# Cross attention's P and V as half-precision pairs, with the products of two heads on the two column halves of the array

## The reference

```python
q = (xn @ w_q).reshape(B, SQ, NUM_HEADS, DIM_HEAD)
kv = context @ w_kv
k, v = jnp.split(kv, 2, axis=-1)
scores = jnp.einsum('bqhd,bkhd->bhqk', q * SCALE, k)
attn = jax.nn.softmax(scores, axis=-1)
out = jnp.einsum('bhqk,bkhd->bqhd', attn, v).reshape(B, SQ, INNER)
out = out @ w_out + b_out
return out * jnp.tanh(gate[0])
```

## Time and profile before

| | |
|---|---|
| median of 3 runs | 815.51 us (809.0 to 815.84) |
| the profiled execution | 821.01 us, its span 819.2 us |
| entries 0 to 7, first score product of each at | 105.4, 165.0, 229.8, 294.6, 359.5, 424.3, 489.2, 554.0 us |
| last product of the attention block, about | 618 us |
| PE, DVE, ACT, POOL busy | 80%, 66%, 50%, 27% of the span |
| granted TensorE clock, mean of the span | 0.895 of 2.4 GHz |

### The profile page before, as it was taken

How to read it: one execution, slowest core, us unless ns; L and a number is a source line. 1 busy time by engine, 2 the same in 40 slices (tenths; PEclk the granted TensorE clock), 3 DMA queues, 4 the chain that set the end, 5 groups by cost and what they waited for, 6 DMA issues and landing times. The chain is left out here.

```text
span 819.2 us, 13429 instructions
## 1 busy us (share of the span) xinstructions
PE 653.4 (80%) x4168; PEld 524.3 (64%) x4168; DVE 540.7 (66%) x1124; ACT 412.3 (50%) x1021; POOL 218.1 (27%) x223
## 2 busy tenths in 40 slices
PE   5717679889889898899889888988767864789980
PEld 4516468678678687777777777867665452456650
DVE  3974367886886787787786787786756851963332
ACT  2414175584585566476466456555533621853431
POOL 3540031231231232132232133122212530133331
PEclk9955689999999999999999999999956986999995
DMA  9113200200110210210210110040216444533324
GB/s 285 46 38 123 62 1 12 77 26 8 56 51 0 61 51 0 61 51 0 51 61 0 37 50 26 11 128 28 78 52 209 144 147 138 174 60 58 53 33 102
DMA packets 55634, 54.24 MB, mean 66 GB/s; under 512 B 17256, under 2 KB 44976, under 8 KB 55600
## 3 DMA queue, kind: packets, MB, share of 16 engines
q1 hardware_dynamic: 51504, 48.61, 19.5%
q0 software_dynamic: 4096, 5.19, 4.0%
HBM read 43.67 MB, written 10.13 MB: 66 GB/s over the span
## 5 line engine op out<-in xcount | busy, mean ns | idle before, releaser
L582 POOL TENSOR_TENSOR probs<-probs,c_rcp 112x750 f32<-112x750 f32 x64 | 92.0, 1437 | 321.3 <-DVE c_rcp L942 321.3
L705 ACT ACTIVATE probs<-ps_s,c_neg 112x375 f32<-112x375 f32 x128 | 72.5, 578 | 30.4 <-DVE c_neg L934 30.1
L1243 PE MATMUL ps_t<-ident,probs 112*125 112x112 f32 x384 | 55.6, 282 | 22.0 <-DVE cpt_lo L946 22.0
L1243 PEld LDWEIGHTS ps_t<-ident,probs 112*125 112x125 f32 x384 | 50.2, 194 | 29.0 <-issue 25.3
L131 PE MATMUL ps_o<-ctxt_hi,w_k_lo 128*128 128x376 f32 x128 | 49.5, 387 | 19.4 <-DVE oct_lo L821 19.2
L613 ACT ACTIVATE kt_hi<-ps_o 128x376 fp32r<-128x376 f32 x64 | 31.4, 490 | 60.8 <-PE ps_o L133 60.8
L1543 POOL DMA_INDIRECT moe_sum<-gsh_hi,xs_in x21 | 33.3, 1585 | 106.3 <-DMA moe_sum<-gsh_hi,xs_in 64.0
L932 DVE TENSOR_REDUCE c_max<-ps_s 112x2 f32<-112x750 f32 x64 | 59.8, 935 | 2.2 <-PE ps_s L133 1.3
L131 PE MATMUL ps_o<-cpt_hi,v_lo 125*128 125x224 f32 x192 | 58.5, 305 | 2.8 <-DVE kt_lo L821 1.7
L946 DVE TENSOR_TENSOR cpt_lo<-ps_t,cpt_hi 125x672 fp32r<-125x672 f32 x64 | 54.7, 855 | 9.0 <-ACT cpt_hi L613 8.9
L613 ACT ACTIVATE oct_hi<-ps_o 64x112 fp32r<-64x112 f32 x128 | 33.0, 258 | 54.4 <-PE ps_o L133 52.9
(11 more groups left out here) (289 smaller groups left out, 1914.7 us busy)
## 6 DMA issues: line engine op xcount, KB each, us to landing
chunk<-in_L_ffn_ew_dram SPq DMA_DIRECT2D x24, 512.0 KB, 3.6
spare<-in_L_ffn_ew_dram SPq DMA_DIRECT2D x18, 512.0 KB
store<-in_L_ffn_ew_dram SPq DMA_DIRECT2D x6, 512.0 KB, 6.0
ctx_raw<-in_ctx_dram SPq DMA_DIRECT2D x8, 375.0 KB
moe_in<-chunk SPq DMA_DIRECT2D x1, 2709.0 KB, 14.1
xs_in<-moe_in SPq DMA_DIRECT2D x21, 129.0 KB
plain_raw<-in_L_xattn_w_kv_dram SPq DMA_DIRECT2D x2, 1024.0 KB, 14.5
store<-in_L_ffn_sw_dram SPq DMA_DIRECT2D x3, 512.0 KB, 6.6
```

The lines of the kernel that those rows point to most:

```text
L582: pool.tensor_tensor(p, p, r, ALU.mult).then_inc(sg["p_normed"], 1)
L705: act.activation(probs[:, s % 2, h, :], ps_s[0:N, h, 0:SK], ACT.Exp, bias=c_neg[:, s % 2, h:h + 1], scale=CROSS_SCALE, accum_out=c_sum[:, ...
L1243: last = pe.transpose(ps_t[0:SKT, h, t * N:(t + 1) * N], probs[:, s % 2, h, t * SKT:(t + 1) * SKT], ident[0:N, 0:N])
```

## The change

P and V of cross attention become pairs of fp16 parts in place of fp32r parts, with the same three products. fp16 has a small range, so the values are scaled by powers of two first. P is multiplied with 2^14 (an immediate of the instructions that split it). V's scale is computed on the chip from a bound on V: the greatest absolute value of V's weights times the greatest sum of absolute values in a piece of the context. `gate_v` takes both scales back out after `cross_out`.

`pv` issues each product by head: 64 columns of stationary V and 112 moving columns of the head's own P. Head 0's go to partitions 0 to 63 of `ps_o`, head 1's to partitions 64 to 127, on the array's column halves. These are 18 matmuls in place of 9, in the order head 0, head 1 for each product. The result is 128 x 112, and `o_hi` and `o_lo` take it out with one instruction each.

To find the scale there are new steps. In the preparation block these are two DMAs of the whole context (3 MB), eight ACT passes over it with sums (125 x 768 each), a DVE maximum over V's raw weights (128 x 2048) and a small one over the sums. At the start of the attention block these are two small transposes and ten small DVE instructions. The V weights are loaded second instead of fifth, and the first projection no longer waits for the second part of x. The preparation block's semaphores are cleared and reused by the later blocks, behind one more meeting of all engines.

```diff
@@ preparation_block
+            load_x(0, slice(0, 2))
+            load_plain(2)
+            load_x(1, slice(2, B))
+            for i in (0, 1, 3):
+                load_plain(i)
             sp.dma_start(raw[:, 6:8, :], ...)
+            for h in range(2):
+                sp.dma_start(ctx_all[:, 12 * h:12 * h + 12, :],
+                             A["ctx"][4 * h:4 * h + 4].rearrange("b (t p) d -> p (b t) d", p=SKT)).then_inc(sg[f"ctx_all{h}"], 16)
...
+            for b in range(B):
+                act.wait_ge(sg[f"ctx_all{b // 4}"], 16)
+                entry = ctx_all[:, ST * b:ST * b + ST, :].rearrange("p t d -> p (t d)")
+                act.activation(entry, entry, ACT.Abs, accum_out=ctx_sum[:, b:b + 1]).then_inc(sg["ctx_sum"], 1)
...
+            dve.wait_ge(sg["plain2"], 16)
+            dve.tensor_reduce(v_cols[:, 1:2], plain_raw[2][:, :], X, ALU.max, apply_absolute_value=True).then_inc(sg["v_cols"], 1)
@@ attention_block
-        v = pair("v", [SKT, 2, ST, 512])
+        v = half_pair(nc, ctx, "v", [SKT, 2, ST, 512])
-        cpt = pair("cpt", [SKT, 2, ST, N])
+        cpt = half_pair(nc, ctx, "cpt", [SKT, 2, ST, N])
...
-                hi(v[0][:, q, t, :], ps_v[0:SKT, :]).then_inc(sg["v_hi"], 1)
+                act.activation(v[0][:, q, t, :], ps_v[0:SKT, :], ACT.Copy, scale=v_scale[0:SKT, 0:1]).then_inc(sg["v_hi"], 1)
...
-                for h in range(2):
-                    r = slice(64 * h, 64 * h + 64)
-                    hi(oct_[0][r, s, :], ps_o[r, h * N:(h + 1) * N]).then_inc(sg["oct_hi"], 1)
+                hi(oct_[0][:, s, :], ps_pv).then_inc(sg["oct_hi"], 1)
...
                 for t in range(ST):
-                    last = product(pe, ps_o[:, 0:2 * N], tuple(w[:, s // 4, t, c] for w in v),
-                                   tuple(w[:, :, t, :] for w in cpt), start=t == 0, stop=t == ST - 1)
+                    for n, (a, w) in enumerate(((1, 0), (0, 1), (0, 0))):
+                        for h in range(2):
+                            at = (s % 4) * P + h * CHD
+                            last = pe.matmul(ps_pv[h * CHD:(h + 1) * CHD, :], v[a][:, s // 4, t, at:at + CHD], cpt[w][:, h, t, :],
+                                             start=t == 0 and n == 0, stop=t == ST - 1 and n == 2)
                 last.then_inc(sg["pv_full"], 1)
...
             preparation_block(nc, signals[0], A, ident, consts, weights, qk_rot, v_all, v_cols)
+            signals[0].clear()
```

More of the change, by code:

```diff
@@ L117, in __getitem__, with clear, release @@
         if name not in self.sems:
-            self.sems[name] = self.ctx.enter_context(self.nc.semaphore(self.block + "_" + name))
+            self.sems[name] = self.nc.alloc_semaphore(name=self.block + "_" + name)
         return self.sems[name]
+    def clear(self):
+        handles = list(self.sems.values())
+        self.nc.clear_and_free_semaphores(handles)
+        self.held = [self.nc.alloc_semaphore(name=f"{self.block}_held{i}", num=h.num) for i, h in enumerate(handles)]
+    def release(self):
+        for h in self.held:
+            self.nc.release_semaphore(h)
 def later(count):
@@ L138, in split_pair, with half_pair @@
     return tuple(ctx.enter_context(nc.sbuf_tensor(f"{name}_{part}", shape, F32R)) for part in ("hi", "lo"))
+def half_pair(nc, ctx, name, shape):
+    return tuple(ctx.enter_context(nc.sbuf_tensor(f"{name}_{part}", shape, F16)) for part in ("hi", "lo"))
 def product_over_width(pe, out, lhs, w, cols):
@@ L146, in product_over_width, with preparation_block @@
     return last
-def preparation_block(nc, sg, A, ident, consts, weights, qk_rot, v_all):
+def preparation_block(nc, sg, A, ident, consts, weights, qk_rot, v_all, v_cols):
     w_k, w_v, w_q, w_o, w_proj = weights
@@ L364, in _ @@
             pe.wait_ge(sg["wt_lo"], 4)
+            project(0, 0)
             pe.wait_ge(sg["x_loaded1"], 16)
-            for b0 in range(B // 2):
+            x_transpose(2, 0)
+            project(1, 1)
+            x_transpose(3, 1)
+            for b0 in range(1, B // 2):
                 if b0 < B // 2 - 1:
@@ L392, in expert_weights, with attention_block @@
     return tuple(A[n][e] for n in ("ew1", "ew2", "ew3"))
-def attention_block(nc, sg, A, x2_all, ident, consts, weights, qk_rot, v_all, raw, ffn_sg, w_max, gw_raw, xs):
+def attention_block(nc, sg, A, x2_all, ident, consts, weights, qk_rot, v_all, raw, ffn_sg, w_max, gw_raw, xs, v_cols):
     w_k, w_v, w_q, w_o, w_proj = weights
@@ L465, in ctx_bank @@
             return bank(f"C{k}") if later(b) else ps_s[:, k, :]
+        ps_k = ps_o[:, 0:SKP]
+        ps_pv = ps_o[:, 0:N]
         stack = work[:, :].rearrange("p (t b r c w) -> p t b r c w", t=2, b=B, r=2, c=4)
@@ L543, in _ @@
         def _(pool):
+            pool.memset(v_mask[:, :], float("inf")).then_inc(sg["masked"], 1)
             pool.memset(chunk[:, 0:D + 1], 0.0).then_inc(sg["zeroed"], 1)
@@ L688, in k_hi @@
                     act.wait_ge(sg["s_full"], PAIRS * b + p - 1)
-                hi(kt[0][:, p % 2, :], ps_o[:, 0:SKP]).then_inc(sg["kt_hi"], 1)
+                hi(kt[0][:, p % 2, :], ps_k).then_inc(sg["kt_hi"], 1)
             def v_hi_cross(b, f):
@@ L711, in cpt_hi @@
                     act.wait_ge(sg["pv_full"], PAIRS * b + s)
-                hi(cpt[0][:, :, :, :].rearrange("p h t n -> p h (t n)"), ps_t[0:SKT, :, 0:ST * N]).then_inc(sg["cpt_hi"], 1)
+                act.activation(cpt[0][:, :, :, :].rearrange("p h t n -> p h (t n)"), ps_t[0:SKT, :, 0:ST * N], ACT.Copy,
+                               scale=P_SCALE).then_inc(sg["cpt_hi"], 1)
             def o_hi(b, s):
@@ L953, in o_lo @@
             def o_lo(b, s):
-                for h in range(2):
-                    dve.wait_ge(sg["oct_hi"], 2 * (PAIRS * b + s) + h + 1)
-                    r = slice(64 * h, 64 * h + 64)
-                    lo(oct_[1][r, s, :], ps_o[r, h * N:(h + 1) * N], oct_[0][r, s, :]).then_inc(sg["oct_lo"], 1)
+                dve.wait_ge(sg["oct_hi"], PAIRS * b + s + 1)
+                lo(oct_[1][:, s, :], ps_pv, oct_[0][:, s, :]).then_inc(sg["oct_lo"], 1)
             def x2_moments(b):
@@ L1203, in k_project @@
                 if later(PAIRS * b + p - 4):
-                    pe.wait_ge(sg["oct_lo"], 2 * (PAIRS * b + p - 4))
+                    pe.wait_ge(sg["oct_lo"], PAIRS * b + p - 4)
                 m = slice(p * P, (p + 1) * P)
                 for k in range(KD):
-                    last = product(pe, ps_o[:, 0:SKP], tuple(t[:, k, m] for t in w_k), tuple(t[:, k, :] for t in ctxt),
+                    last = product(pe, ps_k, tuple(t[:, k, m] for t in w_k), tuple(t[:, k, :] for t in ctxt),
                                    start=k == 0, stop=k == KD - 1)
@@ L1265, in cross_out @@
                     pe.wait_ge(sg["v_lo"], v_before_output(b))
-                pe.wait_ge(sg["oct_lo"], 2 * (PAIRS * b + pairs[-1] + 1))
+                pe.wait_ge(sg["oct_lo"], PAIRS * b + pairs[-1] + 1)
                 for k in pairs:
@@ L1294, in fill @@
                     q_transpose(b, int(f[1]))
-            for f in FILLS[:FILLS.index("T1") + 1] + ["C0", "C1", "O0", "T2"]:
+            pe.transpose(ps_v[0:2, 0:P], v_cols[:, :], ident[:, :]).then_inc(sg["v_scale_full"], 1)
+            fill(0, "QA")
+            fill(0, "QB")
+            pe.wait_ge(sg["v_scaling"], 3)
+            pe.transpose(ps_v[:, P:P + 2], v_row[:, :].to_broadcast([2, P]), ident[0:2, 0:2]).then_inc(sg["v_scale_full"], 1)
+            for f in FILLS[2:FILLS.index("T1") + 1] + ["C0", "C1", "O0", "T2"]:
                 fill(0, f)
+            pe.wait_ge(sg["v_scaling"], 4)
             k_project(0, 0)
```

61 lines of the change are left out of this document (48 added, 13 removed).

## The result

The changed kernel took 792.62 us (median of 4 runs, 789.59 to 796.29) against 812.25 (4 runs, 808.17 to 815.84) for the kernel before: 0.9738 of its time, 95% interval 0.9687 to 0.9789. In a second set it took 792.33 against 816.29, 0.9756 (0.9669 to 0.9844). So it is 20 to 24 us faster. The forecast was 29.3 us and 786; the range 766 to 813 holds the result. The forecast was made off 815.51, the median of three runs. Every ratio in this document is to the kernel before in the same set of runs and leaves out slow runs, those over 1.5% above the fastest of their kernel.

The account below looks back on a forecast made before the run. It took the loop PE (`pv`), ACT and DVE (`oct`), DVE's other work, PE again as the bound. 25.6 + 11.5 - 2.2 - 3.2 + 1.6 - 4 = 29.3 us off 815.5 gives 786; range 766 to 813.

Parts of the forecast that it names:

- the loop PE, ACT, DVE: A step runs through PE (`pv`), ACT and DVE (`oct`), DVE's other work, PE again; the change shortens `pv` and `oct`.
- Both serial rivals: `pv` halves run one after the other: 816, 12%; the same, with weights not loading beside a running matmul: 845, 8%.
- PE: In `pv`, 9 groups at 0.055 plus 0.19 take 0.69 instead of 1.08: 25.6 us saved over 64 pairs.
- 0.19 for the split: Cost in `pv` of going into a split array and moving on to `scores`, both charged: 0.19 us.
- the terms (25.6 - 3.2 + 1.6 = 24.0 of 25.6): `pv` saves 25.6 us, less 3.2 in steps where PE idles, plus 1.6 at entry 7's low clock.
- The way out: Taking `pv`'s result out loses one instruction of 0.27 from the chain; two thirds on the path, 11.5 us.
- The bound of 17.3: Saving on taking the result out if the lost instruction lay on the path in all 64 pairs: 17.3 us.
- One sign named ahead: In the profile after, PE's wait for `oct_lo` would be well under 19 us.
- What gets dearer: In the loop, `v_hi` reads its scale from a tile, 687 ns against 598: -2.2 us; DVE's `lo` charged nothing.
- The start's share of 4: Before the loop, the scale's new steps and the meeting of engines cost 4 us, bounds 0 and 8.
- the 0.8 for the meeting: Before the loop, the cleared semaphores add a meeting of the engines: 0.8 us, taken unseen.
- The step without a gain: In one step of eight PE idles because DVE does the next self softmax before `oct_lo`: -3.2 us.

Follow-up runs that it names:

- the second profile of before: The kernel before, unchanged, run again for another profile: 812.35 us (10 runs), entries of 61.8 us without a low stretch.

## Why the prediction was right, and where it was off

**The mechanism was right**: both halves run at once, the way out is one instruction shorter, and the loop PE, ACT, DVE passes on all of the second and a part of the first. Both serial rivals fell with the timeline. That the profiled spans differ by 29.7, almost the 29.3 forecast, is luck in part: 2.6 of it lies behind attention, and the terms err both ways. By its terms:

- **PE.** 0.055 a group and 0.19 for the split were 0.05 and about 0.13 (the first distance 0.08, the last 0.15), so the block was 0.57 and not 0.69. But at most 0.7 of the saving arrives, where the terms (25.6 - 3.2 + 1.6 = 24.0 of 25.6) had nearly all. By the product 0.51 x 64 x 0.7 = 23 and the two errors cancel; by the entries less arrives, and the term was too large.
- **The way out** was mis-sized: 17 us and not 11.5. The bound of 17.3 was the right value. I had counted PE's waits for `oct_lo`; where PE doesn't wait there, DVE's `cpt_lo` and what follows come earlier instead, and PE waits for those. One sign named ahead did not come: the wait for `oct_lo` was to be well under 19 us, and it is 17.1 (19.2 before), in 21 waits instead of 32. PE comes to it earlier.
- **What gets dearer.** `v_hi` as priced (689 ns for 687). "DVE's `lo` becomes a two-operation form ... I charge nothing" was right of the form and wrong of the scale from a tile, 60 ns. Together with the start it is 8 us by the product, charged were 6.2. The start's share of 4 was right (3.9) as a whole; its parts, the 0.8 for the meeting among them, no run shows.
- **The step without a gain** was there, 12.85 and 12.84. Its reason, DVE's order, was only half of it: ACT's exponentials are late next.
- **Not foreseen:** step 7 gives 0.5 back. The chain `xn`, `xnt_hi`, `xnt_lo` on DVE and ACT didn't get shorter, so PE comes earlier and waits: 1.71 for `xnt_lo`, where the second profile of before has 1.08 (before, then after):

```profile
284.18 0.49 PE L131 MATMUL ps_a<-w_q_hi,xnt_lo 128*112 128x512 f32 x1 [1.08 <-DVE xnt_lo L821]
```

```profile
341.77 0.49 PE L143 MATMUL ps_a<-w_q_hi,xnt_lo 128*112 128x512 f32 x1 [1.71 <-DVE xnt_lo L873]
```

- **The clock is the step that failed.** The prediction priced a low stretch well (1.6, measured 1.5), but took the profiled execution's two an entry for the kernel's own, and then "the steps get shorter as well, so PE's share stays about the same". Before's other profile has fewer, about one an entry, and the mean clock of its runs fits that (0.903, against 0.895 in the first profile); the changed kernel has two. The one in step 4 went, another came in step 7, behind exactly the wait that had grown. That is some 10 us, a good third of what the clock's rival named (26). Without it the change brings 30 to 32 us, against the 29.3 of the sum; with it 20 to 24.

Open is what decides where the stretches fall. The experiments show that filling PE's idle time removes them or moves them, not more. Open too is 2.6 us of the profiled difference after attention (201.6 to 199.0), where the changed code does nothing. Over all profiles, of either kernel and its variants, this stretch varies from 197 to 202 us, so it may be chance.

## What to carry to other kernels

Two independent products with 64 stationary columns each, on the column halves, cost what one does, and the result then lies in one block that one instruction takes out; count in full the instruction that this saves, where it stands in the loop. Compare kernels by span times granted clock beside the time, from several runs, before saying what an edit of 1 or 2% does: here the clock hid a loss of 5 to 8 us once and made another of 17 look like 24. Compare stretches with equally many low ones too, since the product credits a low stretch even where PE waits anyway. When an edit shortens PE's work, look for the wait that grows, and try cheap matmuls in it.
